# Linear attention in pieces of 64 tokens, and the mixture's rounding on ScalarE

## The reference, cut to what matters

```python
q_phi = elu(rope(q)) + 1;  k_phi = elu(rope(k)) + 1        # 16 heads of 8
kv_prefix = cumsum(k_phi[..., :, None] * v[..., None, :])  # over tokens
k_prefix  = cumsum(k_phi)
attn = (q_phi . kv_prefix) / (q_phi . k_prefix + 1e-6)
x = x + sigmoid(gate(delta)) * (attn @ w_o.T)
h = layernorm(x)
gw = softmax(h @ w_moe_gate.T)                              # 4 experts
hid = silu(h @ w1[e] + b1[e]);  eo = hid @ w2[e] + b2[e]
ffn = sum_e gw[e] * eo[e]
```

## Time and profile before

| what | value |
|---|---|
| median of three executions | 1476.04 us |
| the profiled execution | 1480.5 us, its span 1478.7 us |
| busy share of the span: TensorE, VectorE, ScalarE, GpSimd | 86%, 69%, 55%, 48% |
| mean granted TensorE clock, share of full | 0.925 |
| one step of the attention stage, all four batches present | 23.36 and 24.42 us in turn |
| one batch of the mixture, from the fourth on | 26.0 us |

### The profile page before, as it was taken

How to read it: one execution, slowest core, us unless ns; L and a number is a source line. 1 busy time by engine, 2 the same in 40 slices (tenths; PEclk the granted TensorE clock), 3 DMA queues, 4 the chain that set the end, 5 groups by cost and what they waited for, 6 DMA issues and landing times. The chain is left out here.

```text
span 1478.7 us, 33273 instructions
## 1 busy us (share of the span) xinstructions
PE 1266.4 (86%) x10164; PEld 984.0 (67%) x10164; DVE 1013.0 (69%) x3390; ACT 814.8 (55%) x1703; POOL 712.6 (48%) x907
## 2 busy tenths in 40 slices
PE   2899999999986999999999965883988888739998
PEld 1566767676655877777777754773666666539997
DVE  3588888888735899999999984764566666522222
ACT  2355555556426776767777643552556555525554
POOL 3355565656420234343443542335566676426666
PEclk9799999999877999999999986996999999859999
DMA  1101011110102321212112205674111112168872
GB/s 62 40 30 39 31 33 33 31 37 28 45 13 62 69 54 44 64 41 62 40 48 59 73 16 142 196 202 146 27 44 47 49 55 44 44 233 300 266 264 69
DMA packets 70844, 117.53 MB, mean 79 GB/s; under 512 B 9746, under 2 KB 36635, under 8 KB 70768
## 3 DMA queue, kind: packets, MB, share of 16 engines
q1 hardware_dynamic: 58736, 93.49, 21.3%
q0 software_dynamic: 9856, 21.52, 4.6%
q10 hardware_dynamic: 2176, 1.61, 0.4%
HBM read 79.35 MB, written 29.88 MB: 74 GB/s over the span
## 5 line engine op out<-in xcount | busy, mean ns | idle before, releaser
L1159 DVE TENSOR_TENSOR m_Sl<-m_S,m_Sh 128x512 fp32r<-128x512 f32 x256 | 195.5, 769 | 23.3 <-ACT m_S L1076 20.6
L1076 ACT ACTIVATE m_S<-PS,W 128x512 f32<-128x512 f32 x256 | 174.7, 690 | 39.0 <-issue 33.1
L1071 ACT ACTIVATE m_Sh<-PS,W 128x512 fp32r<-128x512 f32 x192 | 132.9, 692 | 72.1 <-PE PS L996 64.5
L1459 POOL DMA_INDIRECT rows<-r_row,r_posi x128 | 131.2, 1025 | 36.2 <-issue 36.0
L761 DVE TENSOR_TENSOR am<-PS,C 128x512 f32<-128x512 f32 x192 | 119.6, 678 | 25.9 <-PE PS L454 25.4
L1693 PEld LDWEIGHTS PS<-f_wt,f_hid 128*128 128x128 f32 x960 | 121.3, 194 | 4.4
L1693 PE MATMUL PS<-f_wt,f_hid 128*128 128x128 f32 x960 | 121.5, 277 | 0.0
L1682 PE MATMUL PS<-f_xT,f_wt 128*128 128x256 f32 x480 | 121.2, 390 | 0.0
L965 POOL TENSOR_TENSOR m_oe<-m_oe 128x512 f32<-128x512 f32 x48 | 67.8, 1412 | 102.2 <-DVE m_oe L1140 101.7
L994 PE MATMUL PS<-m_HH,m_w1h 128*128 128x512 f32 x256 | 107.7, 421 | 7.1 <-DVE m_w1l L1112 4.7
L352 POOL TENSOR_TENSOR am<-am,C 128x512 f32<-128x512 f32 x64 | 81.6, 1275 | 54.8 <-ACT am L636 53.5
(11 more groups left out here) (237 smaller groups left out, 3127.2 us busy)
## 6 DMA issues: line engine op xcount, KB each, us to landing
f_wt<-wr SPq DMA_DIRECT2D x40, 578.0 KB
f_row<-rows SPq DMA_DIRECT2D x40, 260.0 KB
f_wt<-wr SPq DMA_DIRECT2D x40, 256.0 KB, 2.8
m_gb<-gates SPq DMA_DIRECT2D x8, 1024.0 KB, 7.7
m_raw<-gates SPq DMA_DIRECT2D x8, 1024.0 KB, 7.9
f_row<-rows SPq DMA_DIRECT2D x40, 132.0 KB, 2.1
mid<-f_res SPq DMA_DIRECT2D x20, 256.0 KB, 3.3
X<-x SPq DMA_DIRECT2D x16, 256.0 KB, 2.8
```

Source lines behind the costliest of these rows:

```text
L1071: nc.scalar.activation(Sh[:, n % 4, :], PS[:, n % 3, :], ACT.Silu, bias=w("b1")[:, n:n + 1]).then_inc(sh_ready, 1)
L1076: nc.scalar.activation(S[:, n % 3, :], PS[:, n % 3, :], ACT.Silu, bias=w("b1")[:, n:n + 1]).then_inc(s_ready, 1)
L1159: nc.vector.tensor_tensor(Sl[:, n % 4, :], S[:, n % 3, :], Sh[:, n % 4, :].bitcast(F32), ALU.subtract).then_inc(sl_ready, 1)
L1459: nc.gpsimd.indirect_dma_start(out=self.rows, out_offset=bass.IndirectOffsetOnAxis(ap=self.posi[:, u, t:t + 1], axis=0), in_=self.row[:, u ...
```

## The change

The attention stage works on pieces of 64 tokens. The batch keeps its four tiles, but inside a tile only the two 64 x 64 diagonal blocks are scored, and both halves of the array's columns are used: eight products of 8 x 64 weights by 64 columns lie in the array at a time. Two tiles are done in one round, so `scores`, `mask_scores`, `raw_scores`, `mask_last` and `weigh` run twice per batch and not four times, with masks of the same 128 x 512 size. What is carried over comes in seven steps of 64 tokens: `chunks` makes seven k.v sums of 64 tokens one step ahead (for `f`), `mask_chunks` masks them in two VectorE instructions, and `add_chunks` on GpSimd sums them up in six. `turn_k` and `copy_k` move one step ahead too. In `weigh` a carried-over product now stands before each of the four groups `j`. The orders of all engines are changed around this. In the mixture `ROUNDED` becomes empty: ScalarE makes `Sh` and `S` of every chunk.

```diff
-            def mask_last(b, t):
+            def mask_last(b, p):
+                pool.wait_ge(raw_ready, PAIRS * b + p + 1)   # PAIRS = 2
+            def add_chunks(b, first, end):
+                pool.wait_ge(chunks_read, 2 * b + 2)
+                for k in range(first, end):
+                    if k > 1:
+                        pool.wait_ge(state_ready, STATES * b + k - 1)
+                    here = state[:, k % 2, k // 2, :]
+                    nc.gpsimd.tensor_tensor(here, here, state[:, (k - 1) % 2, (k - 1) // 2, :], ALU.add).then_inc(state_ready, 1)
 # GpSimd, steps
                 inverse_deviation(n, ...)
+                add_chunks(b, 1, 3)
                 sum_rotated(f, 0)
-                differences(f, u, c_)
-                sum_rotated(f, 1)
+                add_chunks(b, 3, 5)
                 mask_last(b, 0)
+                sum_rotated(f, 1)
+                add_chunks(b, 5, 7)
+                differences(f, u, c_)
                 keep_x1(b, u)
                 mask_last(b, 1)
                 inverse_deviation(c_, ...)
-                mask_last(b, 2)
                 weigh_keys(f, u)
-                mask_last(b, 3)
 # TensorE
+            def chunks(b, u):
+                pe.wait_ge(ktok_ready, b + 1)
+                after_previous(pe, am_ready, b, 6)
+                for k in range(2 * CT - 1):
+                    t, rows = k // 2, slice(HALF * (k % 2), HALF * (k % 2) + HALF)
+                    mm = nc.tensor.matmul(PS[:, 2 + k % 2, t * P:(t + 1) * P], ktok[rows, t, :], vt[rows, u, t, :], ...)
+            def scores(b, u, p, f):
+                # p: waits for am_ready, raw_ready; p == 0: qk_read(2f+1), chunks_read, ktok_ready, q_stacked, k_stacked
+                for t in (2 * p, 2 * p + 1):
+                    for g in range(4):
+                        for j in range(4):
+                            for half in range(2):
+                                mm = nc.tensor.matmul(PS[half * HALF:half * HALF + HALF, 1 + j, at:at + HALF],
+                                                      kr[rows, u, g, cols], qr[rows, u, g, cols], start=True, stop=True)
+            def weigh(b, u, p):
+                # p == 0: waits for den_step(2b+1); p == 1: for all six states
+                for j in range(4):
+                    # am_ready or last_ready
+                    carried_over(...)      # 128 x 128 weights, 64 columns (two of 32 for j = 2, 3 of p = 0)
+                    for t in (2 * p, 2 * p + 1):
+                        for g in range(4):
+                            for half in range(2):
+                                mm = nc.tensor.matmul(PS[32 * g:32 * g + 32, 5 + half, t * HALF:t * HALF + HALF],
+                                                      vm[rows, u, t, j, 32 * g:32 * g + 32], am[rows, j, at:at + HALF], ...)
 # TensorE, steps: before
-  turn_k(b) gate(c_) scores(b,0) project_out(c_) values(f) update_state(b,0) weigh(b,0) scores(b,1) denominators(b)
-  turn_xn(n) turn_x2(c_) update_state(b,1) weigh(b,1) scores(b,2) pointwise(n) update_state(b,2) weigh(b,2) scores(b,3)
-  turn_z(c_) project(n,"q") logits(c_) weigh(b,3) turn_spread(b) project(n,"k")
 # TensorE, steps: after
+  gate(c_) scores(b,0) denominators(b) project_out(c_) values(f) weigh(b,0) turn_xn(n) scores(b,1) turn_x2(c_)
+  pointwise(n) weigh(b,1) turn_k(f) project(n,"q") turn_z(c_) chunks(f) logits(c_) turn_spread(b) project(n,"k")
 # ScalarE, steps: after
+  gate_tanh(c_) exps(f,0) raw_scores(b,0) exps(f,1) normalise(n) copy_v(f) spread_out(b) copy_xnT(n) raw_scores(b,1)
+  copy_x1(n) copy_k(f) normalise2(c_) scale_h(c_) copy_logits(c_) copy_rdT(b)
 # VectorE, steps: after
+  stats(n) mask_chunks(b) rotate(f,0) divide(c_) rotate(f,1) mask_scores(b,0) phi(f,0) invert(b) close(c_) phi(f,1)
+  mask_scores(b,1) stats2(c_) residual2(c_) prefix(f)
 # mixture
-        ROUNDED = (3,)
+        ROUNDED = ()
```

More of the change, by code:

```diff
@@ L445, in scores @@
                         pe.wait_ge(qk_read, 2 * f + 1)
-                    else:
-                        after_previous(pe, am_ready, b, 12)
-                        after_previous(pe, raw_ready, b, 4)
+                    pe.wait_ge(chunks_read, 2 * b + 2)
+                    pe.wait_ge(ktok_ready, b + 1)
                     pe.wait_ge(q_stacked, COPIES * (b + 1))
                     pe.wait_ge(k_stacked, COPIES * (b + 1))
[L451 to L457, removed]
@@ new lines, in weigh, with carried_over @@
+            def weigh(b, u, p):
+                def carried_over(k, first=0, end=HALF):
+                    t, half = k // 2, k % 2
+                    cols = slice(t * P + half * HALF + first, t * P + half * HALF + end)
+                    return nc.tensor.matmul(PS[:, 5 + half, t * HALF + first:t * HALF + end],
+                                            state[:, (k - 1) % 2, (k - 1) // 2, :], qphi[:, u, cols],
+                                            start=False, stop=False, skip_group_check=True)
+                if p == 0:
@@ L462, in update_state @@
                     pe.wait_ge(den_step, 2 * b + 1)
                 else:
[L464 to L475, removed]
+                    pe.wait_ge(state_ready, STATES * b + STATES)
@@ L476, in weigh @@
                 for j in range(4):
+                    if p == 0 and j in (1, 2):
+                        pe.wait_ge(state_ready, STATES * b + j)
                     if j == 3:
-                        pe.wait_ge(last_ready, 4 * b + t + 1)
+                        pe.wait_ge(last_ready, PAIRS * b + p + 1)
                     else:
[L480 to L485, removed]
+                        pe.wait_ge(am_ready, 6 * b + 3 * p + j + 1)
@@ L535, in steps @@
             def steps(b, u, n, f, c_):
-                if b is not None:
-                    turn_k(b, u)
                 if c_ is not None:
@@ L541, in steps @@
                     scores(b, u, 0, f)
+                    denominators(b)
                 if c_ is not None:
@@ L561, in steps @@
                 if b is not None:
-                    update_state(b, u, 2)
-                    weigh(b, u, 2)
-                    scores(b, u, 3, f)
-                if c_ is not None:
-                    turn_z(c_)
+                    weigh(b, u, 1)
+                if f is not None:
+                    turn_k(f, 1 - u)
                 if n is not None:
@@ L569, in steps @@
                 if c_ is not None:
+                    turn_z(c_)
+                if f is not None:
+                    chunks(f, 1 - u)
+                if c_ is not None:
                     logits(c_)
                 if b is not None:
-                    weigh(b, u, 3)
                     turn_spread(b)
@@ L670, in steps @@
             def steps(b, u, n, f, c_):
-                if b is not None:
-                    copy_k(b)
                 if c_ is not None:
@@ L802, in steps @@
                     stats(n)
+                if b is not None:
+                    mask_chunks(b)
                 if f is not None:
```

145 lines of the change are left out of this document (79 added, 66 removed).

## The result

The changed kernel takes 1573.74 us (median of four, 1571.44 to 1587.93) where the kernel before, run beside it, takes 1473.37. The ratio is 1.0701, interval 1.0633 to 1.0768. The prediction, 1482 with 1446 to 1508, had the sign and missed the size by 92 us. The profiled execution, 1587.93 us, is the slowest of the four; all rows of the changed kernel are from it.

A forecast was written before the change was run, and what follows sets the result against it. Attention was held by TensorE's list, the mixture by VectorE and TensorE; after the change, a loop through ScalarE and GpSimd. +30 full steps, -7 first and last steps, -17 mixture: +6 on 1480.5, adjusted to the median 1482 us, range 1446 to 1508.

The forecast's parts named there:

- The chain: Attention stage: longest loop of waits through TensorE, ScalarE and GpSimd sets a full step, 25.0 us at full clock against 23.36.
- G to X: Attention step from the start of `gate` to that of `turn_xn`: 9.75 us, before 7.6.
- X to Z: Attention step from the start of `turn_xn` to that of `turn_z`: 10.3 us, with TensorE waiting 1.4.
- The faster rival: Attention stage: engine orders don't bind, TensorE's work sets the step at 22 us; total about 1427 to 1440 us; chance 0.13.
- one fall of that length in each step: Attention step: TensorE's clock drops once, about 3.4 us at 1.2 GHz, adding 1.2 us, range 0 to 3.
- Z to G: Attention step from the start of `turn_z` to the next `gate`: 4.95 us.
- the forecast step of 26.2: Full attention step: 25.0 us of chained waits plus 1.2 for low clock, +2.3 against 23.9.
- The last steps: Attention steps with b but no n: 21.6 and 20.3 us at full clock, 1.5 more each for low clock; taken as -7.
- The mixture: Mixture: VectorE loses four copies per batch, so batches take 24.40 us, 1.55 less for each of 12; taken as -17.
- The rival that named ScalarE: Mixture gives nothing because ScalarE, not VectorE, becomes late: 1499 us; chance 0.10.
- eight don't overlap: Attention scores and values: a wave of eight takes 0.107 us, step 28.2, total 1506 us; chance 0.11 with slow starts included.
- The scores round: Attention stage: 128 passes in 16 overlapping waves of eight, 0.057 us each plus 0.15 around them, 1.06 us.

The follow-up runs named there:

- half of the products: Changed kernel with the second half of each tile's score and value products left out in the loop, five useless products added per step: 1511.82 us, ratio 1.0445.
- half tiles: Changed kernel with the second half of each tile's score and value products left out in the loop, nothing added: 1535.13 us, ratio 1.0604.
- the eight-at-a-time variant: Kernel before, with each score product cut into two of 64 rows by 128 columns, eight in the array at a time: 1474.83 us, ratio 1.0188.
- The variant above: Kernel before, with the mixture's rounding on ScalarE and useless products in the attention stage's last three steps: 1436.17 us, ratio 0.9929.
- four variants: Changed kernel with two ScalarE and GpSimd orders put back: alone 1.0693; with useless products 1.0801; also loop written out 1.0694; useless products and half the products 1.064.

## Why the prediction was wrong, step by step

**The chain was the right mechanism, and 1 to 2 us too short.** The prediction's sum at full clock was 25.0 us. A whole step at full clock took 26.53 with half of the products, and 27.6 with all of them when the stall at the jump is taken off (the first step of 26.53 and the one of 29.63 above); both have useless products in them. GpSimd's part is there too. In order of time, ScalarE and GpSimd of the changed kernel, as the earlier trace rows:

```profile
236.54 0.60 ACT L670 ACTIVATE am<-PS 128x512 f32<-128x512 f32 x1 [0.53 <-PE PS L485]
...
237.22 1.27 POOL L356 TENSOR_TENSOR am<-am,C 128x512 f32<-128x512 f32 x1 [5.79 <-ACT am L670]
238.44 1.72 POOL L384 TENSOR_TENSOR rot<-rot 128x512 f32<-128x512 f32 x1
...
240.19 0.63 ACT L661 ACTIVATE ex<-rot 128x512 f32<-128x512 f32 x1 [3.06 <-POOL rot L384]
...
263.67 1.27 POOL L384 TENSOR_TENSOR rot<-rot 128x512 f32<-128x512 f32 x1 [1.01 <-DVE rot L757]
```

The mask stands ahead of the sum and the second exponential waits for both, as foretold. In the step at 264.90 it starts 6.8 us after `gate`, against the predicted 5.9. Half of that is the slow clock under `gate`; the other half is `sum_rotated(f, 1)` itself, which takes 1.71 to 1.73 us in every step of the changed kernel, where the prediction took 1.27 from the step before. `sum_rotated(f, 0)` still takes 1.27 (at 263.67). Why the second one is slower was not tried. So G to X is 10.3 to 10.4 us at full clock in place of 9.75. X to Z ran at full clock in the step at 264.90 and took 11.35 in place of 10.3; the scores round in it took 2.09 in place of 1.06. The faster rival, with TensorE's list free of waits, asked for 22 us a step, and no variant came near it. So the sign was right for its reason: the loop alone, at full clock, is longer than the 23.35 us of the step before.

**The step that failed first: the clock.** The prediction put it as "one fall of that length in each step", and "I take 1.2, and 0 to 3 for the range". There were two or three falls in each step: in the step at 200.1 the clock was low from 4.3 to 7.7, from 14.5 to 17.9 and from 28.2 us on; in the step at 295.4 from 0 to 11.4 and from 28.5 us on. What the 12.6 us of low clock cost is an estimate. At the highest measured rate, 0.49, they are 6.2 us, and at the lowest, 0.2, they are 2.5. What the other causes leave of the 32.1 us is 3 to 5 us (the sum is below), where the term was 1.2 and its upper bound 3. The error in reasoning was to price one fall from the kernel before, where waits were short, although the two last steps of the earlier trace rows already had 0.77 and 0.85, and to find thin products and waits in three places and yet count one fall.

**The term that was missing: instruction fetching.** A pass is two instructions on TensorE, a weight load and a matmul, and the loop's body holds two steps. That is 1300 of them before (no refetching), 1376 with half tiles (none), 1812 in the eight-at-a-time variant (48 fetches in the middle steps) and 2400 now (60). The changed kernel's stalls "issue" of TensorE in 200 to 400 us:

```profile
PE PS L548 <- issue: 5.7, 3, 2.3
PE PS L485 <- issue: 5.6, 6, 1.9
```

11.3 us in 6.25 steps are 1.8 us a step. The variants put the whole effect at about 2.1 us a step in the kernel before, and in the changed kernel at 1.5 with half tiles (fewer passes included) and 1.9 with the loop written out (a higher clock included). The Trainium skill has the mechanism, which I had not drawn on: "Runtime: NRT & Kernel Launch", section "Instruction fetch mechanics", says that instructions are streamed in blocks of 256 and that a jump to a target outside what is held must wait for a fetch. The trace agrees: with the loop written out, nearly as many fetches went with a fifth of the stalls. By count, the 2048 instructions that the same section gives for TensorE would let 1812 fit; the 48 fetches say that this body did not, so the measurement decides. Where between 1376 and 1812 it begins was not tried.

**The sum again, as an estimate.** At full clock and without stalls the step is 26 to 27 us, the 26.53 and 27.6 above with some 0.6 off for the useless products (Z to G is 5.63 with them and was predicted at 4.95). Stalls and fetching add 1.5 to 1.9. What is left of 32.1 is 3 to 5 us for 12.6 us of low clock, 0.25 to 0.37 per microsecond, which lies between the measured rates. So of the 6 us by which the forecast step of 26.2 was short, the clock has 2 to 4, fetching 1.5 to 1.9 and the chain's sizes 1 to 2. The parts are not exact, since a stall taken away comes back in part as a wait.

**The last steps** were to be 7 us shorter (the prediction's own terms, 21.6 + 20.3 + 3 against 50.4, give 5.5) and were 7 longer. Whether 21.6 and 20.3 hold at full clock is not shown, because they ran at 0.67 and 0.50. The variant above shows what the clock alone is worth in such steps: 5 us in two.

**The mixture** was to give 17 and gave 8. The step that failed: "22.54, which is the load of the second batch, and that ran in 24.40 us". VectorE's load came out at 22.8, but the second batch has fewer rounds on ScalarE, 18.20 against 20.9 us now. The wait for the bank's reader, ScalarE, took over. The rival that named ScalarE had the mechanism and too large a price. Two slips elsewhere in the prediction change nothing here: the sum of the rival "eight don't overlap" gives 1508 and not 1506, and the range leaves out all of the first rival's 1427 to 1440.

**The scores round** was to take 1.06 us. At full clock it takes 1.53 (266.33 to 267.86). With about 0.15 around them 128 passes take 1.38 us, 16 waves of 0.086; with half tiles the round of 64 takes 1.09, 16 waves of four in 0.94, which is 0.058 each. So the columns of a wave take what I said, and eight in a wave are not supplied that fast: 10.8 ns a pass. Values come at 7.5 ns a pass (0.38 less 0.14, by 32). Their weights have 32 columns and not 64, but they also come in runs of 32 passes, and the first 32 of a scores round start 7 ns apart as well, but for four longer gaps; the later ones start mostly 8 or 17 ns apart. So the run's length may matter as much as the load, and whether loading or issuing sets the 10.8 was not tried. The rival that the eight don't overlap had 0.107 us a wave; it was wrong too, but half of the way there. The missing 0.5 us lie beside the chain in the first round and on it in the second, and the second, where fetch stalls fall, took 1.9 us or more at full clock. **The values group** was right: 0.70 predicted, 0.75 measured (0.36 carried over, 0.38 for 32 passes).

**What stays open.** Why the clock comes back in some steps and not in others. Waits and thin products are both there whenever it falls; the eight-at-a-time variant clears small tiles with full columns, the useless products show that work in the waits helps, and nothing separates waits from thin products wholly. Whether the stalls "issue" themselves lower the clock is open too. The Trainium skill, "TensorE: Matmul & The Clock Gate", section "A second HAM failure mode: psum-queue depth-cycling", says that short idles between groups of matmuls are enough to make the clock oscillate. The trace agrees that the clock falls again and again, up to three times in 32 us, while TensorE is busy for 29.35 of 32.69 us; that the idles are the reason is not shown here.

## To carry to other kernels

When an edit cuts an engine's work into more and thinner passes with short waits between them, price the clock for each such place, from the worst stretch of the trace and not from the mean one: here it was 2 to 4 of the 6 us a step by which the forecast was short. Count TensorE's instructions in a loop's body before doubling them, and look at the instruction queue in the profile. And an order that frees one product must be followed to the next one in the same list: four variants gave their gain back at the chunks.

## What was unexpected of the hardware

- Matmuls on separate tiles start 6 to 7 ns apart for some 32 passes, but a run of 128 score passes takes 10.8 ns per pass.
- A loop body with 1376 weight loads and matmuls is not fetched again, one with 1812 is at every iteration: about 2.1 us a step of 24, with stalls up to 2.3 us at the jump.
- Adding useless products made a kernel faster: 23 us with half of the products left out (1.0604 to 1.0445), with 5.5 us less of low clock a step; 5 us in the last two steps of the kernel before. In the changed kernel it was 11 us, with overlapping intervals.
- The same instructions took 27.25 and 30.60 us in neighbouring steps of one execution, at 3.4 and 10.2 us of low clock and with the same waits within 0.2 us.
- The same GpSimd addition of 128x512 took 1.27 us in one place of a step and 1.72 in another.
